# Dealing VectorE's work out in single scaling pairs and a mix in 32 steps that reaches into the next batch

## What is computed

```python
cond = einsum('bsi,boi->bso', x, weight[ids])
x_norm = cond * rsqrt(mean(cond * cond) + eps)
H_res = (1 - g) * I + g * sinkhorn((x_norm @ W_res.T).reshape(B, T, 4, 4) + base)
H_pre, H_post = softmax(x_norm @ W_pre.T + ...), softmax(x_norm @ W_post.T + ...)
x_streams = cond.reshape(B, T, 4, 512)
x_pre = einsum('btnc,btn->btc', x_streams, H_pre)
y = x_pre @ W_branch
x_mixed = einsum('btij,btjc->btic', H_res, x_streams)
out = x + (x_mixed + einsum('btc,btn->btnc', y, H_post)).reshape(B, T, 2048)
```

## Time and profile before

| | |
|---|---|
| median of 3 runs | 1799.92 us (1793.94 to 1804.71) |
| profiled execution: time, span | 1800.78 us, 1799.0 us |
| TensorE busy | 1685.7 us (94%), 7690 matmuls |
| VectorE busy | 1505.8 us (84%), 6016 instructions |
| ScalarE, GpSimd busy | 710.0 us (39%), 95.9 us (5%) |
| mean granted TensorE clock | 0.975 of full speed |
| DMA | 237.72 MB, 132 GB/s in the mean |

### The profile page before, as it was taken

How to read it: one execution, slowest core, us unless ns; L and a number is a source line. 1 busy time by engine, 2 the same in 40 slices (tenths; PEclk the granted TensorE clock), 3 DMA queues, 4 the chain that set the end, 5 groups by cost and what they waited for, 6 DMA issues and landing times.

```text
span 1799.0 us, 24465 instructions
## 1 busy us (share of the span) xinstructions
PE 1685.7 (94%) x7690; PEld 1359.2 (76%) x7690; DVE 1505.8 (84%) x6016; ACT 710.0 (39%) x1143; POOL 95.9 (5%) x96
## 2 busy tenths in 40 slices
PE   9999999999999999999999999999999999999704
PEld 7888887787878788787878878787887878787601
DVE  4323589996999879997999969997899969997999
ACT  4334434353343534254343533345342443443503
POOL 0000000000000000000000000000000000000504
PEclk9999999999999999999999999999999999999857
DMA  6323334483245723375244832467233843447002
GB/s 227 94 88 135 129 94 107 117 257 117 89 123 152 236 93 106 94 223 174 93 107 114 255 122 84 117 178 221 94 106 94 247 139 94 112 125 232 1 0 93
DMA packets 65074, 237.72 MB, mean 132 GB/s; under 512 B 7344, under 2 KB 7472, under 8 KB 64816
## 3 DMA queue, kind: packets, MB, share of 16 engines
q1 hardware_dynamic: 56880, 206.80, 34.9%
q0 software_dynamic: 8064, 29.36, 9.2%
HBM read 202.58 MB, written 33.55 MB: 131 GB/s over the span
## 4 chain that ended last, share of the span: by engine, by line
DVE 46%; PE 44%; DMA 4%; SPq 2%; ACT 2%; issue 1%; DVEq 0%; ACTq 0%
PE acc L989 39%; DVE work L807 8%; DVE vec L805 7%; DVE vec L803 7%; DVE w_lo L631 7%; DVE piece L864 5%; DVE xpre L836 3%; DMA x_raw<-xt 2%; DVE x_raw L890 2%; DVE cond_t L669 2%; SPq L219 2%; PE y_ps L1046 2%; DMA w_raw<-wt 2%; PE turn_ps L1004 1%; DVE x_lo L639 1%
## 5 line engine op out<-in xcount | busy, mean ns | idle before, releaser
L989 PE MATMUL acc<-w_hi,x_hi 128*128 128x512 f32 x2048 | 813.0, 397 | 2.8 <-DVE w_lo L631 2.8
L989 PE MATMUL acc<-w_hi,x_lo 128*128 128x512 f32 x2048 | 801.7, 391 | 0.0
L989 PE MATMUL acc<-w_lo,x_hi 128*128 128x512 f32 x2048 | 800.0, 391 | 0.0
L631 DVE TENSOR_TENSOR w_lo<-w_raw,w_hi 128x1024 fp32r<-128x1024 f32 x256 | 312.8, 1222 | 165.6 <-ACT w_hi L388 162.3
L989 PEld LDWEIGHTS acc<-w_hi,x_hi 128*128 128x128 f32 x2048 | 386.3, 189 | 84.6 <-DVE w_lo L631 3.0
L989 PEld LDWEIGHTS acc<-w_hi,x_lo 128*128 128x128 f32 x2048 | 385.7, 188 | 83.2
L989 PEld LDWEIGHTS acc<-w_lo,x_hi 128*128 128x128 f32 x2048 | 386.6, 189 | 78.0
L388 ACT ACTIVATE w_hi<-w_raw 128x1024 fp32r<-128x1024 f32 x256 | 270.3, 1059 | 437.4 <-DMA w_raw<-wt 437.1
L864 DVE SCALAR_TENSOR_TENSOR piece<-cond,kern,piece 128x512 f32<-128x512 f32 x448 | 301.4, 744 | 0.0
L807 DVE TENSOR_TENSOR work<-kern,vec 128x32 f32<-128x32 f32 x1536 | 251.2, 202 | 0.0
L805 DVE RECIPROCAL vec<-vec 128x8 f32<-128x8 f32 x1536 | 242.2, 199 | 0.0
(11 more groups left out here) (110 smaller groups left out, 819.8 us busy)
## 6 DMA issues: line engine op xcount, KB each, us to landing
w_raw<-wt SPq DMA_DIRECT2D x256, 512.0 KB, 3.5
x_raw<-xt SPq DMA_DIRECT2D x64, 512.0 KB, 5.6
piece<-xn POOLq DMA_DIRECT2D x56, 512.0 KB, 6.8
out<-piece SPq DMA_DIRECT2D x56, 512.0 KB, 5.1
x_raw<-xn SPq DMA_DIRECT2D x8, 512.0 KB, 5.6
out<-x_raw SPq DMA_DIRECT2D x8, 512.0 KB, 2.6
cond<-wb SPq DMA_DIRECT2D x1, 1024.0 KB, 14.5
cond<-wall SPq DMA_DIRECT2D x1, 192.0 KB, 12.5
```

The source lines that it names most:

```text
L631: nc.vector.tensor_tensor(w_lo[:, lo, :, :], w_raw[:, lo, :, :], w_hi[:, hi, :, :].bitcast(F32), ALU.subtract).then_inc(w_lo_ready, 1)
L989: mm = nc.tensor.matmul(acc[t][:], stationary, moving, start=(chunk == 0 and m == 0), stop=(chunk == CHUNKS - 1 and m == 2))
```

## The change

VectorE's program is dealt out anew, and the orders that hang on it follow. The number of instructions of arithmetic stays the same on each engine.

- Scaling goes by single pairs (`scale_pairs`), 10 to 22 in a unit, in units 4 to 11 and 13 to 20 (before 5 to 11 and 13 to 19, 18 or 24 in each). The joining wait at each call's end goes; a wait on the chain stands where its result is used.
- The mix goes by terms (`mix_term`, 2 instructions each): 32 steps, one to three a unit in units 21 to 31, and the last four (piece 7) in units 1 and 2 of the next batch. In batch 7 all are done by unit 31 (`MIX_AT_LAST`).
- `pre` is at units 8, 13, 17, 21, its four instructions with single pairs or terms between them; TensorE's turning of x_pre, the branch and ScalarE's spreading shift by one unit for some tiles.
- A store is issued in the iteration after its last term. Piece 7's goes in iteration 3 of the next batch, and the wait for landed stores before `load_x` is gone.

```diff
-FAST_AT = ((5, 12), (13, 20))
-FINAL_AT = 20
-PRE_AT = (8, 12, 16, 20)
+PAIRS = FAST * 6
+PAIRS_AT = {4: 21, 5: 21, 6: 21, 7: 21, 8: 10, 9: 17, 10: 21, 11: 12,
+            13: 12, 14: 19, 15: 22, 16: 19, 17: 10, 18: 22, 19: 19, 20: 21}
+FINAL_AT = 21
+PRE_AT = (8, 13, 17, 21)
...
+MIX_AT = {21: 1, 22: 3, 23: 3, 24: 3, 25: 3, 26: 3, 27: 2, 28: 2, 29: 3, 30: 2, 31: 3, 33: 1, 34: 3}
+MIX_AT_LAST = {21: 1, 22: 3, 23: 3, 24: 3, 25: 3, 26: 3, 27: 3, 28: 3, 29: 3, 30: 4, 31: 3}
...
-            def load_x(b, u, pieces_of=None):
+            def load_x(b, u):
                 place = index(b * PASS_UNITS + u)
-                if pieces_of is not None:
-                    count = index(pieces_of * 2 * 16)
 
                 wait_unit(sp, b - 1, 3 * PASS_UNITS + u)
-                if pieces_of is not None:
-
-                    for slot in range(OUT_SLOTS):
-                        sp.wait_ge(stored[slot], count)
...
                     for q in range(MIX_PAIRS):
-                        slot = q % OUT_SLOTS
-                        if end and U == STORE_AT[q]:
...
+                        if b > 1 and stores_at(False)[q] + 1 == U + UNITS:
+                            store(b - 2, q)
+                        if end and stores_at(last)[q] + 1 == U:
+                            store(b - 1, q)
...
-                def fast_steps(steps):
-
-                    written = [count[0], count[0]]
-                    for _ in range(steps):
...
-                    after(written[1])
+                chain, pairs = [0, 0], [0]
+
+                def scale_pairs(number):
+
+                    for _ in range(number):
+                        if pairs[0] % PAIRS == 0:
+                            chain[:] = count[0], count[0]
+                        side, part = divmod(pairs[0] % 6, 3)
...
+                        for h in range(2):
...
+                            after(chain[h])
...
+                            chain[h] = mark(ins)
...
+                    if U in PRE_AT and U < FINAL_AT:
+                        for j in range(STREAMS):
+                            scale_pairs(1)
+                            pre_term(PRE_AT.index(U), j)
+                        scale_pairs(PAIRS_AT[U] - STREAMS)
+                    else:
+                        scale_pairs(PAIRS_AT.get(U, 0))
...
+                    steps = mix_plan(last).get(U, ())
+                    for place, (q, j) in enumerate(steps):
+                        if U in PRE_AT and place < STREAMS:
+                            pre_term(PRE_AT.index(U), place)
+                        mix_term(c, 1 - parity, q, j)
...
+                    if b > 1:
+                        for q, j in mix_plan(False).get(U + UNITS, ()):
+                            mix_term(c - 1, parity, q, j)
```

More of the change, by code:

```diff
@@ L252, in ending @@
             def ending():
+                store(BATCHES - 2, MIX_PAIRS - 1)
                 load_last_residual(MIX_PAIRS - 1)
@@ L272, in rows, with store @@
                 return t[bass.ds(place, 1), :, :].rearrange("a p (s c) -> (a p) s c", s=2)
+            def store(c, q):
+                sp.wait_ge(mixed, 1 + c * MIX_PAIRS + q + 1)
+                sp.dma_start(rows(out, c * MIX_PAIRS + q), piece[:, q % OUT_SLOTS, :, :]
+                             ).then_inc(stored[q % OUT_SLOTS], 16)
             def body(b, parity, end):
@@ L298, in body @@
                     for q in range(MIX_PAIRS):
-                        slot = q % OUT_SLOTS
-                        if end and U == STORE_AT[q]:
[L301 to L304, removed]
+                        if b > 1 and stores_at(False)[q] + 1 == U + UNITS:
+                            store(b - 2, q)
+                        if end and stores_at(last)[q] + 1 == U:
+                            store(b - 1, q)
                     if not last and U > 3 * PASS_UNITS:
-                        load_x(b + 1, U - 3 * PASS_UNITS - 1,
-                               pieces_of=b if end and U == UNITS - 1 else None)
+                        load_x(b + 1, U - 3 * PASS_UNITS - 1)
                     if last and U > 3 * PASS_UNITS:
@@ L626, in _ @@
         def _(dve):
+            term_written, count = [0, 0], [0]
             def w_low(b, unit):
@@ L768, in log_step @@
                     else:
+                        after(chain[1])
                         ask(tt(vec[:, SUM, :], vec[:, B, :], vec[:, INV, :], ALU.mult))
@@ L823, in final_matrix, with pre_term @@
                         dve.wait_ge(matrix_ready, 1)
-                def pre(t):
-                    if t > 0:
+                weighed = [0]
+                def pre_term(t, j):
+                    if t > 0 and j == 0:
                         dve.wait_ge(pre_turned, c * TILES + t)
[L830 to L842, removed]
+                    weight = logit[:, t, NRES + j:NRES + j + 1]
+                    source = cond[:, 1 - parity, j, t, :]
+                    if j == 0:
+                        weighed[0] = mark(nc.vector.tensor_scalar(xpre[:], source, weight, None,
+                                                                  ALU.mult))
+                        return
+                    after(weighed[0])
+                    ins = nc.vector.scalar_tensor_tensor(
+                        out=xpre[:], in0=source, scalar=weight, in1=xpre[:],
+                        op0=ALU.mult, op1=ALU.add)
+                    if j < STREAMS - 1:
+                        weighed[0] = mark(ins)
+                    else:
+                        ins.then_inc(pre_ready, 1)
                 def pre_low(t):
```

108 lines of the change are left out of this document (49 added, 59 removed).

## The result

| | before | changed |
|---|---|---|
| median of 4 runs each, side by side | 1800.47 us (1793.94 to 1804.71) | **1775.42 us** (1773.69 to 1779.60) |
| ratio | | 0.9869, 95% interval 0.9848 to 0.9889 |
| profiled execution: time, span | 1800.78, 1799.0 us | 1779.60, 1777.8 us |
| mean granted TensorE clock | 0.975 | 0.976 |

The changed kernel is 1.3% faster, 25 us by the medians. That lies in the range and 5 us above the predicted 1770 us; its profiled execution, the slowest of the four, is 8.9 us above the 1770.7 us that the prediction's sum gave for it.

The account below looks back on a forecast made before the run. TensorE, busy 94% of the span, sets the pace, so only its waits can be won. From 1800.8 us, 32.3 less and 2.2 more give 1770.7; by the median, 0.9 lower, 1770 us. Range 1763 to 1784 us (8 in 10).

Parts of the forecast that it names:

- Part 1: Batch boundary: with stores moved and the landing wait gone, TensorE's waits there go, 15.4 us gained.
- A: Batch boundary, units 0 and 1, batches 2 to 7: 8 TensorE waits for the turned low part, 14.1 us.
- That is cover enough: Boundary: weights of unit 3, released by unit 31's end some 7 us before 1039.36, come in time despite the index read.
- Part 2: Units 12 to 20: pairs and x_pre dealt out put VectorE 4.3 us earlier at unit 17; 16.9 us gained.
- B and C: TensorE's waits for the turned low part at unit 18 (7, 12.5 us) and unit 20 (6 of some 0.4 us).
- Part 3: Mix tail in units 1 and 2: slack of 0.12 us at unit 10's projection; 2.2 us lost over batches 2 to 7.
- Part 4: VectorE's joining waits behind pairs: 0.13 us each, counted as gone; not on TensorE's path by themselves.
- Part 5: Ending, batch 7: mix 4.0 us longer in units 30 and 31, cover 1.4 us; loss 0 to 1.5, taken at 0.
- the second: Rival at the boundary: weights still late behind index read and x load, 15.4 us come back, 1785 us; chance 0.1.
- The first: Rival: VectorE's lag in units 4 to 9 is larger, waits at unit 10, 10 us, 1778 us; chance 0.17.
- third: Rival: no net gain, larger lag at unit 10 and boundary waits staying together, about 1796 us; chance 0.06.
- fourth: Rival: VectorE bounds units 4 to 9, a pair costing 0.30 us instead of 0.23; slower, 1809 us; chance 0.05.

Follow-up runs that it names:

- a1: The kernel before, without the wait for landed stores in front of the x load (four lines deleted): 1783.56 us, ratio 0.9909.
- a3: The changed kernel with SyncE's x load of each iteration issued ahead of its stores: 1767.58 us, ratio 0.9820.
- b2: The changed kernel with ScalarE's spreading of piece 7, and so its residual load, in unit 31 instead of 29: 1765.81 us, ratio 0.9817.
- b3: The changed kernel with VectorE's x split of unit 30 behind that unit's mix terms: 1767.76 us, ratio 0.9828.
- a0: The changed kernel run again unaltered, as base of the other runs: 1779.34 us, ratio 0.9884 against the kernel before.
- a2: The kernel before with only the change's pairs and `pre` places; mix in whole pieces, stores and landing wait as before: 1782.13 us, ratio 0.9894.
- c1: a3 with 10 pairs moved from units 9 to 11 into units 4 to 8, two more in each: 1776.43 us, ratio 0.9885.
- c2: a3 with the joining wait put back behind each unit's scaling pairs: 1766.88 us, ratio 0.9826.
- c4: The changed kernel with the edits of a3 and b2 together: 1762.97 us, ratio 0.9808.
- b4: The changed kernel with all mix terms done by unit 31 in every batch, none in units 1 and 2, stores earlier: 1797.74 us, ratio 0.9994.
- c3: b1 with the x loads ahead of the stores, as in a3: 1761.60 us, ratio 0.9797.
- b1: a2 without the landing wait, so no finer mix, no tail and no moved stores: 1763.47 us, ratio 0.9809.

## Why the prediction was right or wrong

The direction and the size came out (1.3% against 1.7% forecast). By steps:

- **What bounds the kernel**: right. The time follows TensorE's waits. From before to after, spans of 1799.0 and 1777.8 us: 18.8 us less of the turned piece's waits, 15 x 0.16 = 2.4 for the waits themselves, 2.0 at the start-up, and 1.7 from one stretch of half clock less inside the batches (last section), against 2.7 + 4 x 0.16 = 3.3 of the new wait. That makes 21.6, where 21.2 were measured. The start-up's 2.0 are not the shorter wait (2.8 to 1.1), for TensorE's work in front of it ended later: the first matmul of the large product starts at 10.04 instead of 10.38, 0.34 us earlier, and the 25th at 15.59 instead of 17.57. The other 1.6 to 1.7 are a stretch at half clock from 11.48 us on, which only the profile of before has there.
- **Part 1 (A gone, 15.4 us)**: this is the step that failed. Its first half holds: the landing wait was worth 16.2 us (a1). The half that failed is "That is cover enough", and with it A taken as gained whole. The changed kernel has 10.1 + 2.7 us and ten waits at the boundary, 14.4 us. I had followed only the weights of unit 3 through the queue. What I hadn't followed was the x load of iteration 29, two iterations earlier, behind a store whose last term had moved, next to two residual loads that the new spreading places put 3.9 us apart (9.1 in the kernel before, at 1004.96 and 1014.07). Three edits that break one link each (a3, b2, b3) bring 11.6 to 13.5 us back against a0. The mark that the prediction set for this part was off too: the weights of unit 3 go out at 1227.45, some 4 us after unit 31's last matmul at 1223.08, not within 1 us, since the index read and the x load in front take 3.6 us; but ScalarE doesn't wait for them.
- **Part 2 (B and C gone, 16.9 us)**: right. a2 alone gives 17.7 us, and no wait is left at units 18 and 20.
- **Part 3 (slack of 0.12 us at unit 10, 2.2 us lost)**: the mechanism is right, the size was on the safe side. Units 4 to 7 take 6.00 each as reckoned. Unit 8 was put at 6.21 us and takes 5.66, as VectorE's timeline of the changed kernel shows, batch 6:

```profile
1282.84 1.22 DVE L650 TENSOR_TENSOR w_lo<-w_raw,w_hi 128x1024 fp32r<-128x1024 f32 x1
...
1288.50 1.21 DVE L650 TENSOR_TENSOR w_lo<-w_raw,w_hi 128x1024 fp32r<-128x1024 f32 x1
1289.63 0.68 DVE L688 TENSOR_TENSOR cond_t<-turn_ps,cond_t 128x512 fp32r<-128x512 f32 x1
1290.23 0.26 DVE L827 RECIPROCAL vec<-vec 128x8 f32<-128x8 f32 x2
```

  That is 0.55 us less, more even than the lower bound of that step allowed for (four times 0.09): an instruction of `pre` costs less here with a pair behind it. The piece is done at 1290.23 and wanted at 1290.89, a margin of 0.66 us, and c1 finds 0.8. It also shows how near the edge it is: 10 pairs earlier cost 9 us.
- **Part 4 (joins)**: the size is right (0.11 to 0.15 us a unit in c2, 0.13 forecast), and so is that TensorE doesn't see it. By the rule of the Trainium skill ("VectorE: DVE Perf Modes", section "The DRAIN you can't avoid") a semaphore behind an instruction costs nothing extra, which the page measured on eight copies. For these small instructions in two chains, where the join makes the next one wait for the last result, the trace doesn't agree; for the kernel's time it makes no difference either way.
- **Part 5 (ending, 0 to 1.5 us)**: right at 0. VectorE's last mix of batch 7 ends at 1637.12, its first work of the ending is at 1638.48, and TensorE waits for the same 1.5 us in two as before. b2 and c4 show what the forecast feared, 1.6 to 2.2 us, with the last residual later.
- **The sum**: 14.4 us more at the boundary, less 2.2 that unit 10 didn't take and 2.0 + 1.7 of the start-up and the clock, give 8.5; the profiled execution is 1779.6 - 1770.7 = 8.9 us above its forecast. The other three runs are 3 to 6 us shorter. The forecast came as near as it did partly by luck: of the 15.4 us of part 1 one was left, and the 3.7 us of the start-up and the clock, which no part of the prediction had, made up for some of it. A batch takes 205.1 to 208.5 us and not the 203 to 204 that were to show the prediction right.
- **Rivals**: the second (A stays, 15.4 us back) happened almost in full in the profiled execution, though not by the mechanism that it named, weights late behind the index read. The first, third and fourth didn't happen: a pair cost the reckoned 0.2314 us in the units read. That the changed kernel still won depends on how its mix is dealt out: without the tail (b4) there was no gain.

## What to carry to other kernels

When work is dealt out finer, the loads and stores that hang on it move too, and every queue that they pass is to be followed for the whole crowded stretch, not only at the place of the old wait. In one in-order queue a load that is due soon goes ahead of a store that waits for compute: that swap of two blocks was worth 12 us with the finer mix, though hardly 2 with the mix in whole pieces (c3 against b1). And take the cheap parts alone before the elaborate one: four deleted lines and the re-dealt pairs and `pre` (b1) gave 36 us, the whole change 20 to 25.

## What the runs showed of the hardware that I had not expected

**TensorE's clock fell to half after some short waits.** TensorE in the changed kernel, behind the wait of 1.90 us at 1232.56:

```profile
1234.57 0.63 PE L1016 MATMUL acc<-w_lo,x_hi 128*128 128x512 f32 x1
1234.99 0.63 PE L1016 MATMUL acc<-w_hi,x_lo 128*128 128x512 f32 x1
...
1236.25 0.40 PE L1016 MATMUL acc<-w_hi,x_lo 128*128 128x512 f32 x1
1236.49 0.39 PE L1016 MATMUL acc<-w_hi,x_hi 128*128 128x512 f32 x1
```

The first two starts are 0.42 us apart, the last two 0.24. By stretches (us, busy and count of each engine, granted clock, DMA share, GB/s), in the same kernel:

```profile
1230.00:1238.00 8.00, 6.11 (x22) 4.42 (x22) 4.01 (x8) 2.55 (x5) 0.00 (x0) 0.79 0.52 185
1238.00:1242.00 4.00, 4.00 (x22) 3.04 (x20) 2.40 (x3) 0.95 (x2) 0.00 (x0) 1.00 0.00 0
```

Of the engine's two levels, 1.2 and 2.4 GHz, the first two rows are at the lower. A granted clock of 0.79 over 8 us is 1.7 us lost. Such a stretch stands right behind three waits of the kernel before (2.77, 1.84 and 3.20 us at 419.76, 942.74 and 1464.24), two of the changed one (1.83 and 1.90), four places of b4, one of a1 (1.85), and two of a2 (2.58 and 2.62), where a longer one begins within the wait of 7.1 us. There is none inside the batches of a3, b1, b2, b3 and c1 to c4. Waits of the same length had none: 1.89 and 1.76 in the earlier trace rows, the six of c1 (1.49 to 1.54), and all six of a0 (1.18 to 1.85), which is the changed kernel itself. So the length of a wait alone doesn't tell which, and one profile doesn't tell how many a kernel has. It is a part of a wait's price that the prediction left out: about 5 us in the profile of before, 3.4 in the first of the changed kernel, none in its second.

**A load's landing time depends on what else is under way.** An x load of 512 KB took a median of 6.1 us in the changed kernel, and 10.0 in the stretch with two accumulating residual loads. It doesn't take two of them: the x load of iteration 29 in the kernel before took 10.0 us beside one residual load, of 10.6 us, and the stores. Whether it is the accumulation or only the bytes that slow it wasn't tried apart.

**Large and small instructions cost less when they alternate.** An instruction of `pre` was 0.69 us from the next of its kind before, where the earlier trace rows give four in 2.76, and cost some 0.55 us net of the pairs between them in unit 8: (5.66 - 1.14 - 10 x 0.2314) / 4.
